# Residual additions of a Mamba and mixture-of-experts kernel as identity matmuls on TensorE, with ScalarE copies

## What is computed

```python
x = x + attn(cond(x))          # attn: Mamba forwards and backwards, out_proj (512 -> 256)
x = x + ffn(cond2(x))          # cond2: x @ w_bot + bias;  ffn: 8 experts, top 2, adds to its own input

def ffn(X):
    logits = X @ Wg + bg                       # top 2 of 8 experts for each token
    out = X
    for e in range(8):
        out = out + where(token chose e, silu(xs @ W1[e]) * (xs @ W3[e]) @ W2[e], 0)
    return out
```

## Time and profile before

| | us |
|---|---|
| median of 3 runs | 1434.04 (1432.5 to 1434.8) |
| the profiled execution: its time | 1436.58 |
| its span | 1434.6 |
| busy: TensorE | 1309.3 (91%) |
| busy: GpSimd | 991.0 (69%) |
| busy: VectorE | 960.0 (67%) |
| busy: ScalarE | 709.1 (49%) |

### The profile page before, as it was taken

How to read it: one execution, slowest core, us unless ns; L and a number is a source line. 1 busy time by engine, 2 the same in 40 slices (tenths; PEclk the granted TensorE clock), 3 DMA queues, 4 the chain that set the end, 5 groups by cost and what they waited for, 6 DMA issues and landing times. The chain is left out here.

```text
span 1434.6 us, 16581 instructions
## 1 busy us (share of the span) xinstructions
PE 1309.3 (91%) x5272; PEld 784.1 (55%) x5272; DVE 960.0 (67%) x1164; ACT 709.1 (49%) x1248; POOL 991.0 (69%) x523
## 2 busy tenths in 40 slices
PE   7899889899997989899887888889999999999997
PEld 3343333343333433333333433446999999999996
DVE  2798999899999999999999899964111111111110
ACT  4787776677776576776677474411111111111111
POOL 1898999999999999999999999833122222222211
PEclk9899999999999999999999999998999999999999
DMA  5544544444445445444554545514988998888992
GB/s 195 178 139 150 146 154 154 146 147 147 147 160 166 150 149 169 149 147 151 173 164 152 170 150 166 173 34 170 359 319 313 322 320 305 322 324 301 324 316 57
DMA packets 103336, 282.45 MB, mean 197 GB/s; under 512 B 9409, under 2 KB 19266, under 8 KB 87762
## 3 DMA queue, kind: packets, MB, share of 16 engines
q1 hardware_dynamic: 95762, 271.17, 54.7%
q0 software_dynamic: 7488, 10.23, 3.3%
HBM read 271.41 MB, written 9.96 MB: 196 GB/s over the span
## 5 line engine op out<-in xcount | busy, mean ns | idle before, releaser
L421 PE MATMUL ps_y<-arena,ident 128*128 128x512 f32 x1024 | 502.0, 621 | 70.4 <-POOL arena L1128 41.4
L1128 POOL TENSOR_TENSOR arena<-arena 128x1024 f32<-128x1024 f32 x184 | 435.7, 2377 | 24.4 <-DVE arena L875 8.7
L421 PEld LDWEIGHTS ps_y<-arena,ident 128*128 128x128 f32 x1024 | 190.9, 195 | 344.7 <-issue 212.6
L1112 POOL TENSOR_TENSOR arena<-arena 128x1024 f32<-128x1024 f32 x128 | 301.6, 2357 | 4.2 <-issue 2.8
L687 ACT ACTIVATE ps_de<-arena,An 128x512 f32<-128x512 f32 x256 | 176.6, 690 | 251.8 <-DVE arena L872 250.9
L1172 POOL DMA_INDIRECT out_x<-arena x39 | 61.8, 1585 | 321.0 <-ACT arena L814 295.9
L859 DVE TENSOR_TENSOR ps_u<-ps_du,arena 128x512 f32<-128x512 f32 x256 | 178.6, 698 | 25.8 <-DVE arena L886 11.5
L1077 DVE TENSOR_TENSOR arena<-ps_du,arena 128x512 f32<-128x512 f32 x39 | 27.0, 692 | 235.1 <-PE ps_du L573 235.1
L687 ACT ACTIVATE arena<-arena,An 128x512 f32<-128x512 f32 x256 | 181.0, 707 | 0.0
L872 DVE TENSOR_TENSOR_SCAN arena<-ps_de,hlast,arena 128x512 f32<-128x512 f32 x128 | 163.0, 1274 | 0.0
L872 DVE TENSOR_TENSOR_SCAN arena<-ps_de,arena 128x512 f32<-128x512 f32 x128 | 155.3, 1213 | 5.3 <-POOL arena L1112 2.9
(11 more groups left out here) (210 smaller groups left out, 1534.6 us busy)
## 6 DMA issues: line engine op xcount, KB each, us to landing
arena<-bc_scratch SPq DMA_DIRECT2D x256, 512.0 KB, 4.6
arena<-in_W SPq DMA_DIRECT2D x117, 1024.0 KB, 8.1
arena<-in_xT SPq DMA_DIRECT2D x2, 1024.0 KB, 5.5
arena<-in_w2c SPq DMA_DIRECT2D x1, 2048.0 KB, 8.6
arena<-in_xT SPq DMA_DIRECT2D x4, 512.0 KB, 6.1
X_scratch<-stg SPq DMA_DIRECT2D x12, 128.0 KB, 4.7
out_x<-stg SPq DMA_DIRECT2D x12, 128.0 KB, 5.0
ipT<-in_ipT SPq DMA_DIRECT2D x1, 1024.0 KB, 8.8
```

The costliest lines, as they stand in the source:

```text
L421: t = e.matmul(Y[j][:, :], ident[:, :], hc[:, i % NP, j, :], start=False, stop=(n == 15))
L1112: e.tensor_tensor(uA[:, turn % 2, :, :], duA.rearrange("p (o t) -> p o t", o=1).to_broadcast([128, 2, TH]), ring[:, turn % NR, 0, :, :], A ...
L1128: e.tensor_tensor(hc[:, i % NP, :, :], hh[:, i % NH, :, :], c, ALU.mult).then_inc(gp_hc, 1)
```

## The change

Out blocks: the four matmuls of each of the six blocks in the loop are followed by an identity matmul of `X[b]` into the same bank, behind a wait for the residual's transfer. ScalarE copies the bank to `X[b]`, three steps after the table's, and VectorE's addition is gone. The two blocks behind the loop stay as they were.

Tiles: X2 is computed twice, into both halves of the bank, and x is multiplied with the identity on top of the second half in place of the transposes. One ScalarE copy takes both halves (512 wide, not 256). VectorE's addition (L910) is gone, and so are the four of GpSimd (L1155). TensorE's transpose of X2 and both stores wait for that one copy.

The core of the diff:

```diff
--- before.py
+++ after.py
@@ -363,9 +363,23 @@
                     else:
                         is_free(("z", b, h, k))
                     t = e.matmul(PS[p][:, :], opT[:, k, mo * 128:mo * 128 + 128], ya[:, k, HB[h]],
-                                 start=(k == 0), stop=(k == 3))
+                                 start=(k == 0), stop=(k == 3 and (b, h) == (1, 0)))
+                if ks[-1] == 3 and (b, h) != (1, 0):
+                    e.wait_ge(l_x, 16 * XT_NO[b, h])
+                    t = e.matmul(PS[p][:, :], ident[:, :], X[b][:, mo, HB[h]], start=False, stop=True)
                 if ks[-1] == 3:
                     t.then_inc(full[p], 1)
+
+            def x2_and_sum(b, cols, p):
+
+                for o in (0, C):
+                    for k in range(2):
+                        e.matmul(PS[p][:, o:o + C], X[b][:, k, cols], wbot[:, b, k, :], start=(k == 0), stop=False)
+                    t = e.matmul(PS[p][:, o:o + C], ones_r, bias2, start=False, stop=(o == 0))
+                for k in range(2):
+                    t = e.matmul(PS[p][:, C + k * 128:C + k * 128 + 128], X[b][:, k, cols], ident[:, :], start=False,
+                                 stop=(k == 1))
+                t.then_inc(full[p], 1)
 
             def tile(b, i, banks):
                 cols = slice(i * 128, i * 128 + 128)
@@ -374,16 +388,11 @@
                 if (b, i) == (0, 4):
                     is_free(("wb", NB - 1))
                 p = take(("x2", b, i), banks)
-                for k in range(2):
-                    e.matmul(PS[p][:, 0:C], X[b][:, k, cols], wbot[:, b, k, :], start=(k == 0), stop=False)
-                e.matmul(PS[p][:, 0:C], ones_r, bias2, start=False, stop=True)
-                for k in range(2):
-                    t = e.transpose(PS[p][:, C + k * 128:C + k * 128 + 128], X[b][:, k, cols], ident[:, :])
-                t.then_inc(full[p], 1)
+                x2_and_sum(b, cols, p)
 
             def tile_T(b, i, banks):
                 sX = tile_buffers(b, i)[1]
-                e.wait_ge(ac_X, TILE_NO[b, i] + 1)
+                is_free(("x2", b, i))
                 p = take(("XT", b, i), banks)
                 for k in range(2):
                     t = e.transpose(PS[p][:, k * 128:k * 128 + 128], sX[:, k * 128:k * 128 + 128], ident[:, :])
@@ -490,12 +499,7 @@
             def last_x2(i):
                 cols = slice(i * 128, i * 128 + 128)
                 p = take(("x2", 1, i), [2, 3, 6, 7])
-                for k in range(2):
-                    e.matmul(PS[p][:, 0:C], X[1][:, k, cols], wbot[:, 1, k, :], start=(k == 0), stop=False)
-                e.matmul(PS[p][:, 0:C], ones_r, bias2, start=False, stop=True)
-                for k in range(2):
-                    t = e.transpose(PS[p][:, C + k * 128:C + k * 128 + 128], X[1][:, k, cols], ident[:, :])
-                t.then_inc(full[p], 1)
+                x2_and_sum(1, cols, p)
 
             for i in range(NU + LAG):
                 if i < NU:
@@ -716,7 +720,11 @@
                 p = is_full(e, ("x2", b, i))
                 if st < 2 and TILE_NO[b, i] >= 2:
                     e.wait_ge(l_st[st], 32 * (TILE_NO[b, i] // 2))
-                e.activation(sX, PS[p][:, 0:C], ACT.Copy).then_inc(ac_X, 1)
+                e.activation(stg[:, st, 0:2, :].rearrange("p w c -> p (w c)"), PS[p][:, :], ACT.Copy).then_inc(freed[p], 1)
+
+            def out_block(b, h, mo):
+                p = is_full(e, ("o", b, h, mo))
+                e.activation(X[b][:, mo, HB[h]], PS[p][:, :], ACT.Copy).then_inc(freed[p], 1)
 
             def tile_T(b, i):
                 st, sX, sB, sT = tile_buffers(b, i)
@@ -781,6 +789,8 @@
                             gate(*GATE_AT[g])
                 if i - 2 in LATE_AT:
                     gate(1, 0, LATE_AT[i - 2])
+                if i - 3 in OUT_AT:
+                    out_block(*OUT_AT[i - 3])
                 if i - 2 in TILE_AT:
                     tile(*TILE_AT[i - 2])
                 if i - 4 in TILE_AT:
@@ -901,14 +911,6 @@
                 e.wait_ge(l_x, 16 * XT_NO[b, h])
                 e.tensor_tensor(X[b][:, mo, HB[h]], PS[p][:, :], X[b][:, mo, HB[h]], ALU.add).then_inc(freed[p], 1)
 
-            def tile(b, i):
-                st, sX, sB, sT = tile_buffers(b, i)
-                p = place["x2", b, i][0]
-                e.wait_ge(ac_X, TILE_NO[b, i] + 1)
-                if st < 2 and TILE_NO[b, i] >= 2:
-                    e.wait_ge(l_st[st], 32 * (TILE_NO[b, i] // 2))
-                e.tensor_tensor(sB, PS[p][:, C:2 * C], sX, ALU.add).then_inc(freed[p], 1)
-
             def tile_top(b, i):
                 tt = b * TPB + i
                 p = place["XT", b, i][0]
@@ -922,10 +924,6 @@
                     second_weights(1)
                 if i in YG_AT:
                     gated(*YG_AT[i])
-                if i - 2 in OUT_AT:
-                    out_block(*OUT_AT[i - 2])
-                if i - 2 in TILE_AT:
-                    tile(*TILE_AT[i - 2])
                 if i - 4 in TILE_AT:
                     tile_top(*TILE_AT[i - 4])
                 if i == at(3, 50):
@@ -1149,10 +1147,6 @@
             def column(v, n):
                 return v.rearrange("p (a o) -> p a o", o=1).to_broadcast([128, NA, n])
 
-            for i in range(4):
-                is_read(e, ("x2", 1, i))
-                x2, xt = xc[0][:, i, 0:C], xc[0][:, i, C:2 * C]
-                e.tensor_tensor(xt, xt, x2, ALU.add).then_inc(gp_sB, 1)
             e.wait_ge(dv_rt, RT["hit"])
             e.tensor_tensor(rhs[:, :, 1, :], hit, column(wt.rearrange("p s a -> p (s a)"), NT),
                             ALU.mult).then_inc(gp_rw, 1)
@@ -1224,9 +1218,8 @@
             def store(b, i):
                 st, sX, sB, sT = tile_buffers(b, i)
                 tt = b * TPB + i
-                e.wait_ge(ac_X, TILE_NO[b, i] + 1)
+                is_read(e, ("x2", b, i))
                 e.dma_start(X_dram[tt * 128:tt * 128 + 128, :], sX).then_inc(l_st[st], 16)
-                is_read(e, ("x2", b, i))
                 e.dma_start(out[tt * 128:tt * 128 + 128, :], sB).then_inc(l_st[st], 16)
 
             keep_rows(0, 0)
@@ -1269,7 +1262,6 @@
                 is_read(e, ("x2", 1, i))
                 e.dma_start(X_dram[T + i * 128:T + i * 128 + 128, :], xc[0][:, i, 0:C]).then_inc(l_st[2 + i], 16)
             for i in range(4):
-                e.wait_ge(gp_sB, i + 1)
                 e.dma_start(out[T + i * 128:T + i * 128 + 128, :], xc[0][:, i, C:2 * C]).then_inc(l_st[2 + i], 16)
             for k in range(4):
                 e.wait_ge(l_st[2 + k], 32)
```

More of the change, by code:

```diff
@@ L212, in build @@
         ac_z = sem("z")
-        ac_X, ac_XT, pe_lg, dv_mx, dv_lg, gp_sB = (sem(n) for n in ("X", "XT", "lg", "mx", "lgt", "gsB"))
+        ac_XT, pe_lg, dv_mx, dv_lg = (sem(n) for n in ("XT", "lg", "mx", "lgt"))
         dv_rt, ac_ex, pe_rx, gp_rw, pe_inv = (sem(n) for n in ("rt", "ex", "rx", "rw", "inv"))
```

## The result

The changed kernel takes 1450.67 us (median of 4 runs, 1444.02 to 1452.83) against 1434.42 us of the kernel before measured beside it: ratio 1.0106, 95% interval 1.0084 to 1.0127. It is 16 us slower; the forecast was 1428.8 us. A later set of runs of the same kernel gave 1457.0 us (ratio 1.0162, 1.0133 to 1.0191). The profiled execution has a span of 1449.1 us, 14.5 us more than before.

The account below looks back on a forecast made before the run. The loop was taken as bound by the slower of VectorE's scan chain and GpSimd's product chain. Loop -4.7 and stage -0.5 gave -5.2 us from the 1434.0 us median: 1428.8 us, own range 1426 to 1431.

Parts of the forecast that it names:

- VectorE gets lighter, 7.4 us: Scan loop: six 128x512 and twelve 128x256 additions leave VectorE, 6 x 0.60 + 12 x 0.32 = 7.4 us.
- ScalarE's copies cost nothing: Loop: six new and twelve longer copies add 6.5 us to ScalarE, which has idle time, so costed at nothing.
- TensorE gets heavier, 1.7 us a tile, 0.9 an out block: Loop: added passes total 5.2 us for out blocks and 20 us for twelve tiles, mostly falling into pauses.
- the first place: At 476.36 us, behind out block (0,1), GpSimd already waits for TensorE; the new pass loses 0.9 us.
- three places: Where TensorE's added work escapes pauses: GpSimd's wait at 476 us, late logits at 730, 792 and 916, TensorE's clock drops.
- I take the two effects as cancelling at 730 and 792: Loop: logits 1.7 us later against some 3 us from avoided clock drops, net nothing; 0.5 us lost at 916.
- Loop -4.7 us: Scan loop in sum: 2.1 us gained until 725, 0 to 792, then 3.1 less 0.5 until 950.
- GpSimd could give 9.6 us back: Loop, 478 to 950 us: GpSimd's waits for VectorE or loads, the most a lighter VectorE can give back.
- Stage, groups +6.8 us: Between loop and experts: four x2 groups lengthen by 4 x 1.7 = 6.8 us, so warm-up ends at 985.8.
- rival A: Slower, 1437.6 us: TensorE late, index matmuls stay at the lower clock (+4.9), loop gives only 1.3; chance 0.13.
- Stage, index matmuls 12.6 to 7.0 us: Before the experts: without a TensorE pause in front, L547's 64 records run at the upper clock, 7.0 us.
- two conditions that I named for a wrong prediction: Loop's last product less than 3 us earlier, or index matmuls taking over 10 us.

Follow-up runs that it names:

- e5: The changed kernel once more, unedited, for a second profile of its loop and groups; 1457.0 us.
- e16: The kernel before with only two warm-up matmuls added in TensorE's pause ahead of the routing matmuls; 1436.81 us, ratio 1.0019.
- e17: The kernel before with only GpSimd's four additions moved behind its product for the index matmuls; 1434.01 us, ratio 1.0004.
- e12: The kernel before with logits ahead of the next x2 group, two warm-up matmuls before routing, GpSimd's four additions behind its index product; 1427.37 us, ratio 0.9949.
- e9: The changed kernel with the last four groups' eight one-row bias matmuls replaced by 128-row ones of the same width; 1438.06 us, ratio 1.0014.
- e2: The kernel before with only the last four tiles changed (doubled x2 groups, no GpSimd additions); 1440.67 us, ratio 1.0043.
- e8: The changed loop with the last four tiles as before, and a tile's logits issued ahead of the next x2 group; 1434.48 us, ratio 1.0000.

## Why the prediction was wrong

- **VectorE gets lighter, 7.4 us.** The additions went away, but VectorE's busy time from 461 us to just ahead of the last scan fell only from 463.8 to 460.3 us in the second profile. 2.0 us of the missing 3.9 are its eight products of step width and input (L848, now L858): 1482 ns in the mean before, 1742 after. The rest I have not traced. A term mis-sized.
- **ScalarE's copies cost nothing.** The copies themselves did not (0.60 us each, as forecast). But I never followed what ScalarE waits for: the sum at 673 us, 2.4 us later because of TensorE, delayed two decays. Partly wrong.
- **TensorE gets heavier, 1.7 us a tile, 0.9 an out block.** The pass of an out block was right (0.86 us), and so was the first place: GpSimd's product at 476.36 us starts 0.8 us later in e5, where I had 0.9. A tile took 2.0 us more (3.8 a group against 1.9), beyond the 1.9 I allowed. The loss was put down to three places. The logits were named rightly, but I set the avoided clock drops against them in full. In the changed kernel the drop at 777 us was gone (the clock from 725 to 800 was 1.00) and VectorE still waited 5.8 us for logits against 3.2. Nor does that drop belong to the code: e16 and e17 have the loop of the kernel before, their clock from 777 to 784 us was 1.00 (0.54 in the trace that I had read), and VectorE waited 0.9 us at the place of the 3.2. The step that failed in the loop is "I take the two effects as cancelling at 730 and 792": the added work of TensorE made VectorE's waits for logits 5.8 us in all, against 1.1 to 3.2 in the traces with the old loop in its old order. The waits for buffers of products and for ScalarE's decays, 1.5 + 0.8 us before and 3.1 + 2.8 in e5, were not in the sum.
- **Loop -4.7 us.** +0.8 in the first trace, +4.5 in the second; the first owes its good look to 3.5 us that it was ahead at step 177. The claim that GpSimd could give 9.6 us back was not tested by anything, since VectorE came no earlier.
- **Stage, groups +6.8 us.** This is the step that failed and decided the time. I priced the groups at the upper level, because those of before mostly ran there. At that level they add 4 x 2.0 us; at the lower one they took 28.9 us, 20.3 more than before. The earlier trace rows had TensorE busy for 10 of 10 us at 0.50; I read it as a matter of the index matmuls, and gave it a chance in rival A, at the wrong place.
- **Stage, index matmuls 12.6 to 7.0 us.** Right: 7.58 us at the upper level, without a pause in front. The reason given, the pause, is not shown: e12 kept the level behind one of 1.69 us.
- **Rival A** had the sign right and the mechanism (the lower level stays while TensorE works) right, with the place and so the size (3.6 instead of 16 us) wrong. Of the two conditions that I named for a wrong prediction, the loop's came true and the index matmuls' did not.

## What to carry to other kernels

Before work is added to TensorE in a stretch that begins after narrow work or a pause, price it at both clock levels. A stretch that is busy without a gap can stay at the lower one: here it did through groups of 28.9 us, and that made 8 us of added work cost 20. When an engine is relieved by giving its work to one that feeds it, list every operation that waits for the feeding engine (logits, buffers to be emptied, sums that a third engine waits for), because each of them moves by the added time. Two repairs of the clock that do nothing alone can pay together, so try them together before they are given up. Before a stall in one trace goes into a sum, look for it in a second trace of the same code: a stall of 3.2 us was 0.9 to 1.7 in others here.

## What was unexpected of the hardware

- TensorE stayed at the lower clock from 964.8 to 1002.4 us while it was busy for 29.5 of 30 us. The Trainium skill (TensorE: Matmul & The Clock Gate, Part 1: The HAM clock gate) puts the level down to "how busy the PE has been recently". By that rule alone the clock would have come back early in the groups; the trace disagrees for the changed kernel's groups, and agrees for e9's and for those of the kernel before.
- Eight matmuls with one row instead of 128 decided in the changed kernel whether the level came back: 28.9 us of groups against 14.9. In other traces it came back in spite of one-row matmuls: at 968.7 us in the kernel before, at 982.6 in e2.
- The same VectorE product of two 128x512 operands (L848) takes 0.69 to 2.31 us in the trace of before, and its mean rose by 18% without any edit to it. What lengthens it was not measured.
- The same code does not meet the clock in the same way twice: the drop at 272 to 279 us, ahead of the first edit, is there in the traces of the kernel before and e5 and missing in those of the changed kernel and e8. The kernel before ranges over 9.6 us.
